# A feed-forward block whose down product runs one chunk later, with a third buffer for the parts of a chunk

## The reference

```python
x = x + attn_a(layernorm(x))      # convolution, running means of q and k, an up and down product with gelu
x = x + ffn(layernorm(x))         # the first feed-forward part: this change is in it
x = x + attn_b(layernorm(x))      # causal attention, 16 heads of 8
x = x + ffn(layernorm(x))         # the second feed-forward part, same weights

def ffn(x):                       # summed over 8 experts of 512 hidden units, all used for every token
    h = silu(x @ Wg[e]) * (x @ Wu[e])
    acc += h @ Wd[e]
```

## Time and profile before

| | |
|---|---|
| median of 3 executions | 1701.44 us (1699.04 to 1702.42) |
| span of the profiled execution, first to last instruction | 1699.8 us |
| PE busy, in the span | 1640.7 us (97%) |
| DVE busy | 1254.7 us (74%) |
| ACT busy | 1054.6 us (62%) |
| POOL busy | 252.8 us (15%) |
| PE's share of the chain that ended last | 82% (DVE 9%, ACT 5%) |

### The profile page before, as it was taken

One profiled execution on the slowest core, in us unless ns is written; L12 is line 12 of the kernel. 1 busy time (PEld: TensorE's weight loads), 2 busy tenths in 40 slices (PEclk: granted clock), 3 DMA queues, 4 the chain that ended last, 5 costly groups with the idle time before them and its releaser, 6 DMA issues.

```text
span 1699.8 us, 28393 instructions
## 1 busy us (share of the span) xinstructions
PE 1640.7 (97%) x10387; PEld 1136.9 (67%) x10387; DVE 1254.7 (74%) x2177; ACT 1054.6 (62%) x1720; POOL 252.8 (15%) x471
## 2 busy tenths in 40 slices
PE   6999999999999999989999999989999999999999
PEld 4667777778777877743333433337888888888887
DVE  6778677777777777788988898865666666666665
ACT  6445765575566555567777777785555555555554
POOL 5522001200110014431211211220000000000000
PEclk9999999999999999999999999999999999999999
DMA  7000002001100033133112122100000000000000
GB/s 223 1 0 1 0 11 53 0 1 38 29 1 0 1 112 111 66 104 95 50 41 64 30 56 57 27 3 1 1 7 7 1 7 7 1 7 1 7 7 7
DMA packets 63443, 52.45 MB, mean 31 GB/s; under 512 B 7999, under 2 KB 58574, under 8 KB 63310
## 3 DMA queue, kind: packets, MB, share of 16 engines
q1 hardware_dynamic: 63136, 50.57, 10.3%
q10 hardware_dynamic: 174, 0.07, 0.0%
HBM read 32.40 MB, written 18.22 MB: 30 GB/s over the span
## 4 chain that ended last, share of the span: by engine, by line
PE 82%; DVE 9%; ACT 5%; issue 2%; POOL 0%; DMA 0%; DVEq 0%; SPq 0%; ACTq 0%; POOLq 0%
PE ps L1311 8%; PE ps L1348 7%; PE ps L1349 7%; PE ps L1350 7%; PE ps L1193 6%; PE ps L1194 5%; PE ps L1195 5%; PE ps L1170 5%; PE ps L1145 4%; PE ps L893 4%; PE ps L1372 4%; PE ps L1373 3%; PE ps L1374 3%; PE ps L1200 3%; PE ps L1202 3%; PE ps L1201 3%
## 5 line engine op out<-in xcount | busy, mean ns | idle before, releaser
L2305 DVE SCALAR_TENSOR_TENSOR hid<-sg,ps 128x512 f32<-128x512 f32 x256 | 175.7, 686 | 184.1 <-PE ps L1350 183.1
L1783 ACT ACTIVATE sg<-ps 128x512 f32<-128x512 f32 x256 | 153.1, 598 | 236.9 <-PE ps L1350 235.2
L1697 ACT ACTIVATE sg<-ps 128x512 f32<-128x512 f32 x256 | 153.3, 599 | 210.3 <-PE ps L1195 205.3
L2168 DVE TENSOR_TENSOR hid<-sg,ps 128x512 f32<-128x512 f32 x256 | 174.8, 683 | 147.0 <-PE ps L1195 104.9
L2158 DVE TENSOR_REDUCE negp<-ps 128x2 f32<-128x1024 f32 (+2 forms) x224 | 249.3, 1146 | 34.5 <-PE ps L1133 17.9
L1691 ACT ACTIVATE pr<-ps 128x1024 f32<-128x1024 f32 (+2 forms) x208 | 196.9, 957 | 62.1 <-PE ps L1133 37.2
L1193 PE MATMUL ps<-xn_hi,w_hi 128*128 128x512 f32 x510 | 209.5, 411 | 0.0
L1348 PE MATMUL ps<-xn_hi,w_hi 128*128 128x512 f32 x512 | 202.4, 395 | 0.0
L1349 PE MATMUL ps<-xn_lo,w_hi 128*128 128x512 f32 x512 | 200.2, 391 | 0.0
L1194 PE MATMUL ps<-xn_lo,w_hi 128*128 128x512 f32 x510 | 200.2, 393 | 0.0
L1195 PE MATMUL ps<-xn_hi,w_lo 128*128 128x512 f32 x510 | 200.1, 392 | 0.0
(11 more groups left out here) (291 smaller groups left out, 3086.2 us busy)
## 6 DMA issues: line engine op xcount, KB each, us to landing
qs<-qd SPq DMA_DIRECT2D x60, 96.0 KB
ks<-kd SPq DMA_DIRECT2D x60, 96.0 KB
kd<-qkp SPq DMA_DIRECT2D x14, 256.0 KB, 2.9
qd<-qkp SPq DMA_DIRECT2D x7, 384.0 KB, 2.6
w_raw<-in_Wg SPq DMA_DIRECT2D x4, 512.0 KB, 7.1
w_raw<-in_Wu SPq DMA_DIRECT2D x4, 512.0 KB, 7.3
w_raw<-in_Wd SPq DMA_DIRECT2D x4, 512.0 KB, 9.0
work<-hd SPq DMA_DIRECT2D x8, 256.0 KB, 4.8
```

Of the source, the lines that this page charges most:

```text
L2305: v.scalar_tensor_tensor(hid[:, q % 4, :], sg[:, q % 2, :], 2.0, bank(up_bank(q)), ALU.mult, ALU.mult).then_inc(f["prod"], 1)
```

## The change

`down` is moved one step later on PE: step k now issues `gate_up` of chunk k+2 and then `down` of chunk k-1. Step 0 issues no down product, and the last step of the last tile issues two, one before and one behind the first attention products. The waits of `down` move into the function with it. Since two chunks' parts are now alive while a third is made, `h_hi` and `h_lo` get three buffers, indexed by `k % 3`. The copy of bank 4 to `yS` moves from the first step of a tile to the second (`c == DOWN_LAG`), behind the last down product of the tile before. The scratch memory that the launcher reserves for software DMA is set to 1024, which makes room for the two new buffers (4 KB per partition together).

```diff
+H_BUFS, DOWN_LAG = 3, 1
...
-        h_hi = sb("h_hi", [P, 2, NT], F32R)
-        h_lo = sb("h_lo", [P, 2, NT], F32R)
+        h_hi = sb("h_hi", [P, H_BUFS, NT], F32R)
+        h_lo = sb("h_lo", [P, H_BUFS, NT], F32R)
...
-                def down(h, c):
-                    w = slice(c * P, (c + 1) * P)
+                def down(q):
+                    t, c = divmod(q, CH)
+                    pool_rests = rests_by_pool(q - LAST_PAIR)
+                    w, at = slice(c * P, (c + 1) * P), q % H_BUFS
                     dst = bank(4)
...
+                    pe.wait_ge(f["hhi"], q + 1)
+                    if q - LAST_PAIR in REST_BY_POOL:
+                        pe.wait_ge(f["hlo_pool"], pool_rests)
+                    else:
+                        pe.wait_ge(f["hlo"], q + 1 - pool_rests)
+                    if c == 0:
+                        pe.wait_ge(f["y_out"], t + 1)
+                    pe.matmul(dst, w_hi[2][:, w], h_hi[:, at, :], start=(c == 0), stop=False)
+                    pe.matmul(dst, w_hi[2][:, w], h_lo[:, at, :], start=False, stop=False)
+                    mm = pe.matmul(dst, w_lo[2][:, w], h_hi[:, at, :], start=False, stop=(c == CH - 1))
...
                                 gate_up(h if c + 2 < CH else 1 - h, (c + 2) % CH)
+                            if k >= DOWN_LAG:
+                                down(k - DOWN_LAG)
                             if end and c == CH - 1:
...
                                 next_max(0, 0)
-                            pe.wait_ge(f["hhi"], k + 1)
...
-                            if c == 0:
-                                pe.wait_ge(f["y_out"], t + 1)
-                            down(h, c)
+                                down(k)
...
-                            a.copy(h_hi[:, c % 2, :], hid[:, c % 4, :]).then_inc(f["hhi"], 1)
-                            if c == 0:
+                            a.copy(h_hi[:, k % H_BUFS, :], hid[:, c % 4, :]).then_inc(f["hhi"], 1)
+                            if c == DOWN_LAG:
                                 act.wait_ge(f["y_done"], t + 1)
                                 a.copy(yS[:], bank(4)).then_inc(f["y_out"], 1)
...
-    nc = bacc.Bacc("TRN2", target_bir_lowering=False, num_devices=1)
+    nc = bacc.Bacc("TRN2", target_bir_lowering=False, num_devices=1, dynamic_dma_scratch_size=1024)
```

More of the change, by code:

```diff
@@ L845, in ffn_beside_sequences @@
                     if p in REST_BY_POOL:
+                        h_at = (LAST_PAIR + p) % H_BUFS
                         pool.wait_ge(f["hhi"], LAST_PAIR + p + 1)
-                        g.tensor_tensor(h_lo[:, p % 2, :], hid[:, p % 4, :], h_hi[:, p % 2, :].bitcast(F32),
+                        g.tensor_tensor(h_lo[:, h_at, :], hid[:, p % 4, :], h_hi[:, h_at, :].bitcast(F32),
                                         ALU.subtract).then_inc(f["hlo_pool"], 1)
@@ L1195, in gate_up @@
                         pe.matmul(dst, w_lo[m][:, w], xn_hi[:, h, :], start=False, stop=True).then_inc(f[sig], 1)
-                def down(h, c):
-                    w = slice(c * P, (c + 1) * P)
+                def down(q):
+                    t, c = divmod(q, CH)
+                    pool_rests = rests_by_pool(q - LAST_PAIR)
+                    w, at = slice(c * P, (c + 1) * P), q % H_BUFS
                     dst = bank(4)
-                    pe.matmul(dst, w_hi[2][:, w], h_hi[:, c % 2, :], start=(c == 0), stop=False)
-                    pe.matmul(dst, w_hi[2][:, w], h_lo[:, c % 2, :], start=False, stop=False)
-                    mm = pe.matmul(dst, w_lo[2][:, w], h_hi[:, c % 2, :], start=False, stop=(c == CH - 1))
+                    pe.wait_ge(f["hhi"], q + 1)
[8 more added lines that the diff above has]
+                    mm = pe.matmul(dst, w_lo[2][:, w], h_hi[:, at, :], start=False, stop=(c == CH - 1))
                     mm.then_inc(f["y_done"] if c == CH - 1 else f["dn"], 1)
@@ L1261, in pair @@
                                 next_max(0, 0)
-                            pe.wait_ge(f["hhi"], k + 1)
-                            if last and p in REST_BY_POOL:
-                                pe.wait_ge(f["hlo_pool"], rests_by_pool(p))
-                            else:
-                                pe.wait_ge(f["hlo"], k + 1 - (rests_by_pool(p) if last else 0))
-                            if c == 0:
-                                pe.wait_ge(f["y_out"], t + 1)
-                            down(h, c)
+                                down(k)
                             if c == 3:
@@ L1712, in pair @@
                             else:
-                                act.wait_ge(f["dn"], (TILES * (CH - 1)) - 1)
+                                act.wait_ge(f["dn"], (TILES * (CH - 1)) - 1 - DOWN_LAG)
                             act.wait_ge(f["prod"], k + 1)
-                            a.copy(h_hi[:, c % 2, :], hid[:, c % 4, :]).then_inc(f["hhi"], 1)
-                            if c == 0:
+                            a.copy(h_hi[:, k % H_BUFS, :], hid[:, c % 4, :]).then_inc(f["hhi"], 1)
+                            if c == DOWN_LAG:
                                 act.wait_ge(f["y_done"], t + 1)
@@ L2188, in pair @@
                                 dve.wait_ge(f["hhi"], k + 1)
-                                v.tensor_tensor(h_lo[:, c % 2, :], hid[:, c % 4, :], h_hi[:, c % 2, :].bitcast(F32),
+                                v.tensor_tensor(h_lo[:, k % H_BUFS, :], hid[:, c % 4, :],
+                                                h_hi[:, k % H_BUFS, :].bitcast(F32),
                                                 ALU.subtract).then_inc(f["hlo"], 1)
```

## The result

The changed kernel takes 1686.53 us (median of 4 runs, 1685.87 to 1687.65), the kernel before on the same chip 1701.83 us (4 runs, 1699.04 to 1702.42). The ratio is 0.992, 95% interval 0.9904 to 0.9936: 13.6 us less, between 10.9 and 16.3; the medians themselves differ by 15.3 us. One later execution of the kernel before, 1815.55 us at a mean clock of 0.85, was in a slower state of the chip and is left out of all medians and ratios. Two further comparisons gave 0.9919 (0.9905 to 0.9932) and 0.9917 (0.9901 to 0.9932). The forecast was 1690.0 with a range of 1686.5 to 1696.5, so the time lies at the very end of the range, 0.03 us inside it.

What follows compares the result with a forecast made beforehand. PE was taken as the bound from 62 to 740 us (busy 98.7%), with only its late starts to win: 14.4 - 0.25 - 1.3 - 0.95 - 0.3 - 0.2 = 11.4 us, giving 1690.0 us, range 1686.5 to 1696.5.

Steps and rivals of the forecast that it cites:

- the 14.4 us by starts: First feed-forward part, down's late starts: 11.6 us at 36 places plus 2.8 us for the matmuls after; at most 14.4 us.
- k = 7: Longest late start of down, with ACT in gelu and a table load before the high part: all 1.65 us won.
- k = 11 to 14: First pair, k = 11, 13, 14: gains 1.75 us, T1 and conv take back 1.3, about 0.45 us stay.
- The signs: Down without waits for the low part, 0.23 us behind up at 36 places; PE's waits for gate and up stay absent.
- all won: Rival: all 14.4 us of down's late starts won, none given back, 1687 us; chance 0.08 for below 1687.5.
- T1 by the yS copy, minus 0.95: Middle pairs, k = 65 and 129: the moved copy delays ACT's tokens, T1 starts no sooner; 0.95 us given back together.
- T10, minus 0.3: Middle pairs: one T10 loses the copy in front, the next gets it; 0.15 us given back per pair, 0.3 together.
- spread of 1.7 us for the clock: Clock dip behind the first feed-forward part, at the start of attention: 1.7 us either way, not in the sum.
- Most comes back: Rival: gains return as attn_a waits, 5.1 us remain, 1696.3 us; chance 0.21 for 1693 to 1698.
- DVE as the bound: Rival: DVE needs more per step than PE, waits move to the product, no change, 1701 us; chance 0.08.
- The copy stalls PE: Rival: first down product of each of 8 tiles waits for the yS copy, 5.2 us slower, 1706.6 us; chance 0.03.

Runs made afterwards that it cites:

- wait_kept: The changed kernel, but PE waits for the high and low part of chunk k ahead of down(k - 1): 1699.57 us, ratio 1.0001 to the kernel before.
- copy_late: The changed kernel with the yS copy on ACT behind the attn_a pieces of step c = 1, all pairs but the last: 1689.85 us.
- between: The changed kernel with down(k - 1) between the gate and the up product of its step instead of behind both: 1702.95 us.
- ahead: The changed kernel with down(k - 1) ahead of gate and up of its step, behind the attn_a pieces: 1712.34 us.
- copy_at_zero: The changed kernel with the yS copy on ACT at c = 0, where it stood before the change: 1693.93 us.

## Why the prediction was right

**The wait was the cost, and starts were its measure.** wait_kept shows it: the same order without the room loses 10.9 of the 12.9 us again. The page's idle time for down's waits, 6.0 us, was half of what was won; the 14.4 us by starts were within 1.3 us of the 13.1. k = 7 gave 1.65 us, as forecast; k = 11 to 14 gave 0.37, forecast 0.45; the first pair 4.7, forecast 4.8; the last 1.2, forecast 0.9. The signs came as well: no down product starts late any more, and no wait for gate and up appears.

**The number was helped by luck.** 1686.53 lies below the narrower range of the forecast, 1687.5 to 1693, and where the prediction had put "all won", at 0.08. But not all was won. A gain 1.7 us larger than forecast and some 1.8 us from outside the part came together, and with 0.03 us less the time would have been outside the range.

**The terms that were mis-sized** are two give-backs of the middle pairs, where 3.5 and 3.7 us were won and 2.8 and 2.9 forecast.

- *T1 by the yS copy, minus 0.95.* At k = 65 and 129 0.29 us each were kept at T1, and the next step won its 0.39 in full. The step "whose end goes from 248.07 to about 248.57" counted the copy twice: ACT's token half ended at 246.72 + 0.87 = 247.59, and 248.07 was already that with the copy added. T1 had the 0.3 us to gain that DVE's half, done at 248.21, allows, not nothing. In the profile after, ACT's tokens end at 241.02, DVE's at 241.16, and T1 starts at 241.21: it is DVE's half that it comes behind, not ACT's, as the prediction had given for a sign.
- *T10, minus 0.3.* The first T10 of a pair lost its wait and the second kept it, a gain of about 0.2 us per pair by starts, where I had charged 0.15. The copy had stood just ahead of L1580. After, on ACT and PE:

```profile
316.19 1.51 ACT L1587 ACTIVATE work<-ps,lna 128x128 f32<-128x128 f32 x4
...
318.44 0.60 PE L896 MATMUL ps<-ident,work 128*128 128x128 f32 x4
```
It is done 0.7 us before PE comes. That wait_kept keeps 1.47 us in the middle pairs points to the same. So the middle pairs won 3.5 us where down's own late starts came to 3.4: part of what came there was never down's wait, and offset what T1 and `ntok` gave back.

Against these stands a give-back that I missed: the transposes of `ntok`, 0.03 and twice 0.13 us later by starts, 0.3 in all. Their chain on DVE hangs on the up product, as the run with down between gate and up showed.

**The rest of the difference** lies outside the part. The forecast went from 1701.4, the median of three runs; 62 later runs of the kernel before gave medians of 1699.7 to 1700.6, so some 1.3 us of it are the base (in the comparison of the result the kernel before still took 1701.83, and the changed kernel won 15.3). Against the profile of before, whose start was a late one, the first profile of the changed kernel also had 1.65 us at the start and the absent dip behind the part. Its spread of 1.7 us for the clock was in the prediction; that the start-up has one too was not: the first gate product of k = 0 comes at 63.63 us in the profile of before, 60.13 with only the buffers, 60.63 to 61.98 in those of the changed kernel. I take the gain as 12.4 to 13.1 us by the marks; the ratios give 13.6 to 14.1 us, which their intervals can't tell from it.

**The rivals.** Most comes back: no, 13.1 of 14.4 stayed. DVE as the bound: no; waits for the product stayed absent and DVE still waits 96.4 us for PE; with the stalls gone the matmuls still follow each other in 0.23 us. The Trainium skill (TensorE: Matmul & The Clock Gate, Back-to-back issue gap) states 131 ns, and the trace after disagrees with it as the trace before did. The copy stalls PE: not in this form, but I gave it 0.03 from one place at which the copy waited for PE, without working out its slack in the new order. At two tiles there is none beyond the 0.15 us of the release, and copy_late shows 3.9 us for a copy behind one more piece. The case was nearer than the prediction knew.

**What was not foreseen at all** is what between and ahead show. The prediction treated down's place as a matter of down's own operands. It also sets how long PE is busy between an up product and the next wait on what DVE and ACT do behind its product. The change happened to leave that distance alone (down stays behind up), and only so could its gain be read off down's waits: luck of the design, not a step of the prediction.

## What to carry to other kernels

When an engine works in order, a block that is moved changes two distances: from its operand's producer to it, which is the wait one wants to remove, and from the last release that other engines depend on to the next wait on their results, for which it was filler. Work out both before moving it; 0.69 us less of filler after each up product, with the late copy that came with it, cost 15.7 us here, more than the change wins. Price a stall by starts against the undisturbed spacing, not by the idle time shown. And compare stretches between two marks of the same work: these repeat to 0.3 us where medians differ by 1 to 2, as long as the granted clock between the marks is the same, which has to be looked up.

## What the runs showed of the hardware

- The profile's idle time understates each late start, as the earlier trace rows let expect, now borne out: 6.0 us shown, 10.9 us lost again when only this wait was put back. A matmul after a late start is followed by the next after 0.31 us instead of 0.23.
- At the down products a release takes effect 0.14 to 0.15 us after the end of the releasing ACT or DVE instruction (copy end 240.24, down 240.39; in copy_late 241.05 and 241.19), at T1 and T10 only 0.05 us after it (DVE's tokens end 241.16, T1 241.21; in copy_at_zero ACT's end 327.82, T10 327.87). So a wait without idle time in the profile can still be the one that sets the start.
- The lower clock level can follow a wait of PE of 2 us, and need not. In "down ahead" PE stood idle 1.90 us before down at 244.75, and from 246.0 to 249.4 us the clock was at 1.2 GHz; the step took 4.58 us. The same wait of 1.90 us before down at 413.26 was followed by full clock, and the step took 2.97. With the copy at c = 0 a wait of 2.08 us before 489.42 was followed by the low level from 490.8 us, the same wait before 324.98 was not.
- Eleven executions of copy_at_zero range from 1693.18 us at a mean clock of 0.998 to 1701.29 at 0.991. The low clock comes and goes at the same work from run to run. Between 33 and 48 us the mean granted clock was 0.66 in the profile of before, 0.77, 0.89 and 0.89 in those of the changed kernel, 0.89 with only the buffers; the dip behind the part was absent in two of the three profiles of the changed kernel and there in the third:

```profile
33.00:48.00 15.00, 12.36 (x39) 7.44 (x40) 11.56 (x51) 10.33 (x13) 11.72 (x8) 0.66 0.01 2
```
(the stretch of before; columns as in the earlier trace rows)
